# Four passes over 32 images on one core: the normalisation factors of the second and fourth pass go to all channels by transfer instead of by matrix product

## What is computed

```python
def layernorm(x, w, b, eps=1e-05):
    mu = jnp.mean(x, axis=-1, keepdims=True)
    var = jnp.var(x, axis=-1, keepdims=True)
    return (x - mu) * jax.lax.rsqrt(var + eps) * w + b
xn = layernorm(x, ln1_w, ln1_b)
...  # roll by 3, windows of 7 x 7, six heads: softmax(q k * scale) v, projection
x = shortcut + o
h = layernorm(x, ln2_w, ln2_b)
h = jax.nn.gelu(h @ mlp_w1 + mlp_b1, approximate=False)
x = x + (h @ mlp_w2 + mlp_b2)
```

## Time and profile before

| | us |
|---|---|
| median of 3 runs | 11,815.78 |
| lowest, highest | 11,811.32, 11,822.69 |
| the profiled execution | 11,807.14 |
| its span in the profile | 11,805.3 |
| PE busy in the span | 11,116.6 (94%) |
| ACT, DVE, POOL busy | 7,831.3 (66%), 7,378.2 (62%), 5,227.8 (44%) |
| mean granted clock of PE | 0.977 |

### The profile page before, as it was taken

One profiled execution on the slowest core, in us unless ns is written; L12 is line 12 of the kernel. 1 busy time (PEld: TensorE's weight loads), 2 busy tenths in 40 slices (PEclk: granted clock), 3 DMA queues, 4 the chain that ended last, 5 costly groups with the idle time before them and its releaser, 6 DMA issues. The chain is left out here.

```text
span 11805.3 us, 397033 instructions
## 1 busy us (share of the span) xinstructions
PE 11116.6 (94%) x158740; PEld 8317.4 (70%) x158740; DVE 7378.2 (62%) x12642; ACT 7831.3 (66%) x13524; POOL 5227.8 (44%) x6916
## 2 busy tenths in 40 slices
PE   6999999899999999998989999998999999999999
PEld 2444444577777777777767777776888888788887
DVE  4444444577777777775447777776666666666665
ACT  4555555477777777776337777775777777777776
POOL 0000000377777777775014544443555555555554
PEclk9999999899999999999989999998999999999999
DMA  1111111122222222222643333332010000010100
GB/s 54 39 40 36 40 35 40 33 53 50 52 51 51 51 52 51 51 51 77 216 146 80 81 79 79 80 79 54 24 25 24 25 24 24 25 25 25 24 24 22
DMA packets 1105622, 617.63 MB, mean 52 GB/s; under 512 B 864651, under 2 KB 1076566, under 8 KB 1099704
## 3 DMA queue, kind: packets, MB, share of 16 engines
q1 hardware_dynamic: 1091496, 553.66, 19.3%
q10 hardware_dynamic: 12288, 38.54, 1.0%
HBM read 308.38 MB, written 282.75 MB: 50 GB/s over the span
## 5 line engine op out<-in xcount | busy, mean ns | idle before, releaser
L1484 POOL TENSOR_TENSOR L_HdL<-L_Hd,L_HdH 128x392 fp32r<-128x392 f32 x1536 | 1572.7, 1024 | 283.8 <-POOL L_HdH L1482 283.1
L1468 POOL TENSOR_TENSOR L_SQ<-L_X 96x392 f32<-96x392 f32 x512 | 428.5, 837 | 2298.8 <-DMA L_X<-after_L 2288.6
L991 PE MATMUL banks<-L_ident,L_PR 113*113 113x113 f32 x9216 | 1201.1, 267 | 1.2 <-DVE L_X L1390 0.7
L991 PEld LDWEIGHTS banks<-L_ident,L_PR 113*113 113x113 f32 x9216 | 1143.1, 180 | 63.8 <-DVE L_X L1390 9.8
L1219 ACT COPY L_PT<-banks 113x452 f32<-113x452 f32 x1792 | 885.8, 538 | 371.1 <-PE banks L991 369.2
L1235 ACT ACTIVATE L_PR<-L_SX 113x588 f32<-113x588 f32 x1536 | 1088.0, 708 | 52.3 <-DVE L_SX L1362 10.3
L1482 POOL CAST L_HdH<-L_Hd 128x392 fp32r<-128x392 f32 x1536 | 785.1, 511 | 740.5 <-issue 658.1
L395 PE MATMUL banks<-scan_XS,scan_W1T 97*96 (+1 forms) x2688 | 1111.4, 552 | 0.0
L1054 PE MATMUL banks<-L_VB,L_PT 113*49 113x34 f32 x36864 | 1064.1, 213 | 2.0 <-ACT L_PT L1219 1.0
L1262 ACT ACT_TABLE_LOAD x512 | 656.9, 1283 | 607.3 <-PE banks L998 607.2
L1356 DVE TENSOR_REDUCE L_MX<-banks 113x12 f32<-113x588 f32 x1024 | 783.4, 765 | 432.2 <-PE banks L1037 432.2
(11 more groups left out here) (239 smaller groups left out, 27006.6 us busy)
## 6 DMA issues: line engine op xcount, KB each, us to landing
L_X<-after_L SPq DMA_DIRECT2D x768, 147.0 KB
after_L<-L_X SPq DMA_DIRECT2D x512, 147.0 KB
conv_T<-L_norm_by_phase SPq DMA_DIRECT2D x96, 512.0 KB, 3.3
L_norm_by_phase<-L_XP SPq DMA_DIRECT2D x512, 84.0 KB, 2.1
scan_XT<-in_x SPq DMA_DIRECT2D x33, 1176.0 KB, 7.1
L_norm<-L_XA SPq DMA_DIRECT2D x256, 147.0 KB, 1.9
L_conv<-conv_D ACTq DMA_DIRECT2D x96, 392.0 KB, 3.0
L_XR<-L_norm SPq DMA_DIRECT2D x256, 147.0 KB, 2.6
```

The source lines that it names most:

```text
L991: mm = pe.transpose(bank(TURN[a])[0:SPAN, (k % 4) * SPAN:(k % 4 + 1) * SPAN], PR[:, st.v if lag else st.u, 2 * k:2 * k + 2, :].rearrange(" ...
L1484: pool.tensor_tensor(HdL[:, u, j].bitcast(F32R), Hd[:, u, j], HdH[:, u, j], ALU.subtract).then_inc(s[f"hd_parts_{j}"], 1)
```

## The change

The matrix product `spread`, its constant `PICK` and its event are gone. ACT issues, right behind the Exp, one transfer per norm: row 32 g of `RS`, one partition, is read 96 times and written to the 96 partitions of a new tile `RB` in SBUF. Each is 147 KB (96 x 392 x 4 bytes); there are three in a step of L1 and two in a step of L3. `normalised` waits for the landing and multiplies by `RB`. On PE the variances stand between the first two parts of `output` and the scores ahead of `hidden`; on ACT both `probs` stand ahead of `SQ2`, `values_even` ahead of `XN2H`, and the table of Gelu is loaded ahead of the wait for the first layer; on DVE `values_odd` stands ahead of `normalised` and both `centre` ahead of `residual`. The diff, cut:

```diff
-                    for g in range(C // NORM_ROWS):
-                        dve.memset(PICK[NORM_ROWS * g:NORM_ROWS * g + 1], 1.0)
...
+        spread_rows = [[sem(f"spread{g}{u}") for u in range(2)] for g in range(3 if kind == "L1" else 2)] if mlp else []
@@ PE, variances
-                    if kind == "L1":
-                        st.wait("xh", 5)
-                    else:
+                    st.wait("lv", 0)
+                    if kind == "L3":
                         st.wait("y", 4)
@@ PE
-                def spread(st):
-
-                    st.wait("rstd", -1)
-                    for k in range(PAIRS):
-                        cols = slice(2 * TOK * k, 2 * TOK * (k + 1))
-                        for g, _ in norms(st):
-                            rows = slice(NORM_ROWS * g, NORM_ROWS * (g + 1))
-                            mm = pe.matmul(bank(NORM_BANK[g])[0:C, cols], PICK[rows], RS[rows, st.u, cols], start=True, stop=True)
-                    mm.then_inc(s["spread"], 1)
@@ PE, scores
-                        if st.ahead().f:
-                            st.wait("xn", -1)
-                        if third_norm(st):
-                            st.wait("xh", 4)
+                        st.wait("lv", -1)
@@ ACT, rstd
+                    for g in present:
+
+                        st.wait(("xn", "xn2", "xh")[g], (1, 4, 6)[g])
                     for rows in parts:
                         ins = act.activation(RS[rows, st.u], LV[rows, st.u], ACT.Exp, scale=-0.5)
                     ins.then_inc(s["rstd"], 1)
+                    st.wait("rstd", -1)
+                    for g in present:
+                        act.dma_start(RB[:, g, st.u], RS[NORM_ROWS * g:NORM_ROWS * g + 1, st.u].unsqueeze(1).broadcast_to([1, C, CH])).then_inc(spread_rows[g][st.u], 16)
@@ DVE, normalised
-                    st.wait("spread", -1)
                     if st.m:
-                        dve.tensor_tensor(XN2[0:C, st.u], x1_of(st, 2)[0:C], bank(NORM_BANK[1])[0:C, 0:CH], ALU.mult).then_inc(s["xn2"], 1)
+                        st.wait_turn(spread_rows[1][st.u], 2, 1)
+                        dve.tensor_tensor(XN2[0:C, st.u], x1_of(st, 2)[0:C], RB[:, 1, st.u], ALU.mult).then_inc(s["xn2"], 1)
...
-                        dve.tensor_tensor(XH[:, st.u], X2[0:C, st.u], bank(NORM_BANK[2])[0:C, 0:CH], ALU.mult).then_inc(s["xh"], 1)
+                        st.wait_turn(spread_rows[2][st.u], 4, 1)
+                        dve.tensor_tensor(XH[:, st.u], X2[0:C, st.u], RB[:, 2, st.u], ALU.mult).then_inc(s["xh"], 1)
@@ DVE, mlp_step
+                    if st.f:
+                        values_odd(st)
                     if normed:
                         normalised(st)
-                    if st.f:
-                        values_odd(st)
                     if st.k:
                         over_sums(st)
                     if st.f:
                         centre(st, 0)
+                        centre(st, 1)
                     if st.k:
                         residual(st)
-                    if st.f:
-                        centre(st, 1)
```

More of the change, by code:

```diff
@@ L734, in window_pass @@
         if mlp:
-            J = sb("J", [C, NORM_ROWS]); PICK = sb("PICK", [C, C])
+            J = sb("J", [C, NORM_ROWS]); RB = sb("RB", [C, 3 if kind == "L1" else 2, 2, CH])
             SQ = sb("SQ", [C, 2, CH]); SQ2 = sb("SQ2", [C, 2, CH]); LV = sb("LV", [C, 2, CH]); RS = sb("RS", [C, 2, CH])
@@ L778, in window_pass @@
             loads += [(gb[:, 0:1], column(p["dw_b"]))]
-        load_all(nc, kind, loads, zeros=zeros, values=[(J[:], 1.0 / C), (PICK[:], 0.0)] if mlp else [])
+        load_all(nc, kind, loads, zeros=zeros, values=[(J[:], 1.0 / C)] if mlp else [])
         with nc.Block() as block:
@@ L828, in window_pass @@
             names += ["xn_high", "xn_parts", "xn2_high", "xn2_parts"]
-            names += ["sq", "sq2", "variances", "lv", "rstd", "spread", "xn2", "fc2", "x2"]
+            names += ["sq", "sq2", "variances", "lv", "rstd", "xn2", "fc2", "x2"]
             names += [f"fc1_{j}" for j in range(HB)] + [f"gelu_{j}" for j in range(HB)]
@@ L852, in window_pass @@
         K_BANK, Q_BANK = (7, 3) if mlp else (3, 6)
-        VAR_BANK, NORM_BANK = 2, (0, 1, 2)
+        VAR_BANK = 2
         TOKEN_BANK = (2, 6)
@@ L1109, in mlp_step @@
                         output(st, 0)
+                    if normed:
+                        variances(st)
+                    if st.n:
                         output(st, 1)
@@ L1113, in mlp_step @@
                         turn(st, 0)
-                    if normed:
-                        variances(st)
                     if st.n:
@@ L1124, in mlp_step @@
                         turn(st, 2)
-                    if normed:
-                        spread(st)
                     if st.f:
@@ L1135, in mlp_step @@
                         heads(st)
+                    if st.f:
+                        scores(st)
                     if st.m:
@@ L1145, in mlp_step @@
                         hidden(st, 1)
-                    if st.f:
-                        scores(st)
                     if st.k:
@@ L1195, in _ @@
                     variances(first)
-                    spread(first)
                 over_chunks(pe, s, mlp_step if mlp else attention_step, LAST)
@@ L1201, in _ @@
                 LOG_EXP = "natural_log_exp_and_others"
+                GELU = "gelu_and_others"
                 def rstd(st):
@@ L1245, in mlp_step @@
                         pt_copy(st, 2)
+                    if st.f:
+                        values_even(st)
                     if st.m:
@@ L1257, in mlp_step @@
                     if st.m:
+                        act.preload_act_table_set(GELU)
                         st.wait("hd_parts_2", 4)
@@ L1271, in mlp_step @@
                         probs(st, 0, 0)
+                        probs(st, 1, 0)
                     if st.k:
@@ L1276, in mlp_step @@
                         act.activation(SQ2[:, st.v], x1_of(st, 1)[0:C], ACT.Square).then_inc(s["sq2"], 1)
-                    if st.f:
-                        probs(st, 1, 0)
                 def front(st):
@@ L1397, in normalised @@
                     nx = st.ahead()
-                    st.wait("spread", -1)
                     if st.m:
-                        dve.tensor_tensor(XN2[0:C, st.u], x1_of(st, 2)[0:C], bank(NORM_BANK[1])[0:C, 0:CH], ALU.mult).then_inc(s["xn2"], 1)
+                        st.wait_turn(spread_rows[1][st.u], 2, 1)
+                        dve.tensor_tensor(XN2[0:C, st.u], x1_of(st, 2)[0:C], RB[:, 1, st.u], ALU.mult).then_inc(s["xn2"], 1)
                     if nx.f:
                         nx.wait_turn(loaded[nx.of4(0)], 0, N_LOADS, 4)
-                        dve.tensor_tensor(seen(XN[0:C, nx.u]), win(X[0:C, nx.of4(0)]), win(bank(NORM_BANK[0])[0:C, 0:CH]), ALU.mult).then_inc(s["xn"], 1)
+                        nx.wait_turn(spread_rows[0][st.u], 0, 1)
+                        dve.tensor_tensor(seen(XN[0:C, nx.u]), win(X[0:C, nx.of4(0)]), win(RB[:, 0, st.u]), ALU.mult).then_inc(s["xn"], 1)
                     if st.m:
```

4 lines of the change are left out of this document (1 added, 3 removed).

## The result

| | before | after |
|---|---|---|
| median, us | 11,818.98 (4 runs) | 18,402.39 (4 runs) |
| lowest, highest | 11,811.32, 11,822.69 | 18,399.58, 18,409.47 |
| span of the profiled execution | 11,805.3 | 18,407.7 |
| mean granted clock of PE | 0.977 | 0.767 |

The ratio after to before is 1.558, with a 95% interval of 1.556 to 1.560: the changed kernel takes 6,583 us more. The forecast was 19,700 us, with 15,000 to 21,300 as its range.

What follows compares the result with a forecast made beforehand. PE's list was taken as the bound. Steps growing from 12.63 to 30.0 us and 13.77 to 27.2 us, 256 each, added 4,447 and 3,438 us to 11,807; with 9 us to the median, about 19,700 us, range 15,000 to 21,300.

Steps and rivals of the forecast that it cites:

- The source: New transfers, each reading one partition: at 24 GB/s one takes 6.3 us, against 0.75 us at 201 GB/s.
- the grey image: Existing single-partition transfer in the trace, 22 to 24 GB/s, taken as the model for the new transfers' rate.
- my second rival: New transfers: larger pieces flow at twice the rate, 48 GB/s, 3.1 us each; 15,140 us in all; chance 0.06.
- In a row or beside: Transfers of one step counted one after another: 18.8 us in the second pass, 12.5 us in the fourth.
- Rival 1: Second pass: third transfer runs beside the others, 6.3 us less per step, 18,090 us in all; chance 0.13.
- The common order of the queue: All sixteen DMA engines take their shares in issue order, so the transfers follow one another; argued against the third overlapping.
- The chain behind the landing: From one variances product to the next, through the transfers: 28.7 us in second pass, 24.9 in fourth, at full clock.
- the clock: PE's clock falls towards half in its pauses; half the loss counted, 1.3 us a second-pass step, 2.3 a fourth-pass step.
- The sum: Both passes, 256 steps each: +4,447 us and +3,438 us on 11,807 us, with 9 us to the median about 19,700.
- The issues: Three transfer issues on ACT, 0.32 to 0.95 us each, counted as nothing because ACT is idle in the following wait.
- The gain that would be there: Removed spread products on PE, 0.91 us per step in both passes: 466 us saved if nothing else changed.
- Rival 3: One source is no obstacle, but a chain from SQ2 through the variances gives 13.4 us steps, 12,190 us; chance 0.12.

Runs made afterwards that it cites:

- e7_quarter: The changed kernel with each transfer moving only the first 98 of 392 columns, from the same single partitions; 13,657.90 us, ratio 1.156.
- e3_rows_apart: The changed kernel with the three transfers reading rows 0, 36 and 72 instead of 0, 32 and 64; 17,052.24 us, ratio 1.443 to before.
- e2_copy96: The changed kernel with each transfer reading the 96 partitions of RS instead of one partition 96 times; 12,317.05 us, ratio 1.043 to before.
- e1_order_only: The changed kernel's order of all engines, but the factors still spread by the matrix product, without transfers; 12,715.83 us, ratio 1.076 to before.

## Why the prediction was right, and where its terms were off

**The source.** Right, and the term that decided. I had taken 24 GB/s from the grey image; 147 KB at the measured 26 to 29 GB/s are 5.2 to 5.8 us, not 6.3. The pieces' size, my second rival, has little part in it: pieces seven times larger raise 24 to 29 GB/s at most, and those of e7_quarter flow at 18 to 24.

**In a row or beside.** Half right. In the fourth pass two transfers take 12.7 us from issue to landing, where the sum had 0.81 + 12.5 = 13.3. In the second pass the first two take 13.4 us, as counted. That is partly luck: the bytes of each flowed faster than counted, but the first landed 7.8 us behind its issue, 1.4 us more than 0.81 + 5.6, a time at its ends that I had put at nothing. The third lands 3.3 us behind the second, not 6.3: partition 64 is partly served while 32 is. Rival 1 wanted it wholly hidden and steps of 22 to 24 us; the steps are 26.1 to 27.0. Its mechanism is real (e3_rows_apart). The common order of the queue, which I held against it, is a likely reason why it gives only a part; no run separates it.

**The chain behind the landing.** Right within 1 us. The step shown, from the end of one variances product (5002.80) to the next: 1.24 us to the issue (counted: 1.20), 16.76 to XH (counted: 19.6), and 8.1 from XH to the next variances (counted: 7.9 at full clock and 1.3 for the clock). The clock lay between its two levels as I said: 0.60 over the step ahead of this one and 0.74 in this one. But the rest of the step was 0.2 us longer than counted at full clock here and 0.9 us in the step ahead, not 1.3. The timeline shows why the two differ: here SQ2 on ACT ends at 5027.90 and the variances begin at 5028.00, so ACT's list sets the end; in the step ahead SQ2 ends at 5001.06 and PE, at 0.53 us for each product of L1075 instead of 0.34, comes to the variances only at 5001.69. In the fourth pass the rest of the step is 25.94 - 1.24 - 12.68 = 12.0 us, counted 12.7 (10.4 and 2.3 for the clock).

**The sum.** 256 x (26.5 - 12.63) + 256 x (25.94 - 13.77) = 3,551 + 3,116 = 6,667 us, and the spans differ by 6,602. The forecast had 7,885. Of the 1,283 us between, 896 are in the second pass (30.0 counted, some 26.5 measured), 323 in the fourth (27.2 against 25.94), and the other 64 in the steps at the ends of the passes. The term that was most off in size is the third transfer "in a row": XH could run 16.8 us behind the first issue, not 19.6, which is 2.8 of the 3.5 us in the second pass; the rest is the clock, 0.2 to 0.9 us for 1.3. The rate of 24 GB/s, too low by itself, made no difference there, for the first two landed as counted. In the fourth pass the two landings give 0.6 of the 1.3 us and the chain behind them the rest.

**The issues.** I counted nothing for them, and this was wrong in itself though hidden here. Three issues hold ACT for 3.83 us, and `pt_copy` behind them is late by that, so that PE's heads wait 2.88 us. All of this lies beneath the wait for the landing. With the fast source it shows: in e2_copy96 the issues take 1.81 us.

**The gain that would be there.** I had 466 us for the products, if nothing else changed. From e1_order_only to e2_copy96 they bring 399 us. That is no clean measurement, since the wait of the scores for XH goes at the same time and waits for landings come in its place (330.7 us in front of XN2).

**Rival 3** was the best description of what is left without the slow source: a step of 13.4 us and 12,190 us in all, by a chain from SQ2 to the variances. e2_copy96 has steps of 13.5 us in most of the second pass and 12,317 us, and putting SQ2 back gives 247 us. But it named a single chain, and the ladder has three more terms that I had at nothing or below. The earlier variances alone cost 166 us. The two `values` ahead add 398 us together in the old banks. And the early table load, of which I wrote that it saves nothing in the new step, is worth 187 us in the old one: right as written, and I had not asked what it does alone.

**Still open.** Why the third issue is held: two take 1.18 us together, three take 3.83, and in e2_copy96 three take 1.81. A queue that is full until the first transfers drain would look like this, but no run separates it. e2_copy96 changes two things at once, the partitions that are read and that the same bytes are read 96 times; a transfer that reads different bytes of one partition was not run, and only e3_rows_apart speaks for the partition. `values_odd` and `values_even` were not moved apart. And how much of e1_order_only's loss is left once the banks are free was not run.

## What to carry to other kernels

Before a transfer inside the chip replaces an instruction, count the partitions that it reads: bytes, target and number of DMA engines were the same in two kernels here, and one source partition against 96 made a median of 12.0 us to landing against 2.5. Ask of a wait on the busiest engine what it does to the clock too, since PE's work behind a pause of 2 us ran at 0.57 in e7_quarter. And try the small parts of a bundle alone: the one line that loads a table ahead of a wait made the kernel 1.6% faster, in a bundle that was 56% slower.

## What the runs showed of the hardware

- Sixteen DMA engines that all read one SBUF partition move 26 to 29 GB/s together, at a busy share of 0.85 to 0.93. The same engines at about the same share (0.86, 0.89) move 250 to 268 GB/s when the new transfers read 96 partitions, other loads and stores included.
- The busy share of the DMA engines is no measure of what they move: 0.54 with 42 GB/s after, 0.23 with 51 before.
- Transfers from one partition each run beside one another when the partitions are apart in the right way: with 0, 36 and 72 their queue moves 48 GB/s over 6 us, with 0, 32 and 64 it moves 26 over 10 us. At the start it is 26 to 29 in both.
- Issuing a transfer from SBUF to SBUF costs the issuing engine about 0.6 us, on ACT (0.61) as on SP (0.59), where a store issued by SP took 0.32; three in a row on ACT can hold it for 3.83 us, of which the third has 2.63.
